# Causal attention: a group's queries and keys loaded in two column halves, each with its own semaphore

## What is computed

```python
xn = _layernorm(x, axis=-1)
s = _L0_attn_ref(xn, ...)          # 16 heads of 16 numbers, causal softmax over all 2048 keys
g = _silu(_L0_ffn_ref(xn, ...))    # two layers with a local window of 128
x = x + s * g
```

```python
scores = jnp.einsum('bhqd,bhkd->bhqk', qc, k) * scale
scores = jnp.where(causal_mask[None, None], -jnp.inf, scores)
m = jnp.max(scores, axis=-1, keepdims=True)
p = jax.nn.softmax(scores - m, axis=-1)
oc = jnp.einsum('bhqk,bhkd->bhqd', p, v)
```

## Time and profile before

| | us |
|---|---|
| median of 3 runs | 4747.14 |
| lowest, highest | 4740.44, 4750.38 |
| the profiled execution's own time | 4743.15 |
| its span, first to last instruction | 4741.2 |
| PE busy | 4448.3 (94%) |
| DVE busy | 3586.0 (76%) |
| ACT busy | 2997.1 (63%) |
| mean granted TensorE clock | 0.972 of full |

### The profile page before, as it was taken

The page is one execution under the profiler, slowest core; times in us unless marked ns, Lnnn a source line. Parts: engine busy times, 40 slices in busy tenths (PEclk is TensorE's granted clock), DMA queues, the critical chain, the costliest instruction groups (busy, mean ns, idle before and its releaser), DMA issues. The chain is left out here.

```text
span 4741.2 us, 92153 instructions
## 1 busy us (share of the span) xinstructions
PE 4448.3 (94%) x32224; PEld 2968.1 (63%) x32224; DVE 3586.0 (76%) x7576; ACT 2997.1 (63%) x6873; POOL 1420.6 (30%) x1940
## 2 busy tenths in 40 slices
PE   8589999999999999699999999999999999999976
PEld 7433443443443433477777777777777777777756
DVE  7488888888888885577777777777777777777736
ACT  3157777777776778366666666665666666666632
POOL 3112222222222122433333334333333333333300
PEclk9789999999999999799999999999999999999999
DMA  8833344433333430200000000010100000000008
GB/s 299 240 45 57 56 90 72 76 59 53 57 64 65 77 65 25 76 23 19 23 15 19 23 19 23 19 50 14 66 20 19 24 19 23 19 23 15 19 13 283
DMA packets 186991, 268.79 MB, mean 57 GB/s; under 512 B 75860, under 2 KB 126764, under 8 KB 179644
## 3 DMA queue, kind: packets, MB, share of 16 engines
q1 hardware_dynamic: 186556, 263.12, 22.5%
HBM read 157.62 MB, written 104.87 MB: 55 GB/s over the span
## 5 line engine op out<-in xcount | busy, mean ns | idle before, releaser
L725 ACT ACTIVATE a_pt<-a_ring 128x512 f32<-128x512 f32 (+3 forms) x2560 | 1180.5, 543 | 438.8 <-PE a_ring L849 421.1
L776 DVE TENSOR_REDUCE a_mx<-a_ring 128x2 f32<-128x1024 f32 (+3 forms) x1079 | 1116.6, 1064 | 244.1 <-PE a_ring L869 118.3
L1136 POOL TENSOR_TENSOR l_rn<-l_ssm,l_half 128x8 f32<-128x8 f32 x256 | 447.8, 1749 | 832.9 <-DVE l_ssm L1386 832.9
L862 PE MATMUL a_ring<-a_ks,a_qs 48*128 48x512 f32 (+3 forms) x2560 | 555.6, 430 | 94.5 <-DMA a_ks<-qk_d 60.9
L849 PE MATMUL a_ring<-a_qs,a_ks 49*128 49x512 f32 (+3 forms) x2560 | 560.2, 445 | 57.9 <-ACT a_pt L725 29.8
L886 PE MATMUL a_ot<-a_pt,a_vt 128*32 128x512 f32 (+3 forms) x5120 | 602.1, 549 | 2.0 <-ACT a_os L731 1.3
L849 PEld LDWEIGHTS a_ring<-a_qs,a_ks 49*128 49x128 f32 x2560 | 248.2, 187 | 464.1 <-ACT a_pt L725 270.8
L1235 ACT ACTIVATE l_pr<-l_pr,l_negm 128x256 f32<-128x256 f32 (+1 forms) x1024 | 501.3, 495 | 7.4 <-DVE l_negm L1438 6.6
L667 POOL TENSOR_TENSOR a_gate<-a_gate 128x1 f32<-128x1 f32 x512 | 99.6, 195 | 1281.4 <-ACT a_pt L725 1271.4
L862 PEld LDWEIGHTS a_ring<-a_ks,a_qs 48*128 48x128 f32 x2560 | 258.1, 191 | 346.2 <-ACT a_pt L725 173.7
L1243 ACT ACTIVATE l_pts<-l_banks 128x512 f32<-128x512 f32 (+1 forms) x512 | 298.6, 583 | 208.7 <-PE l_banks L1705 138.4
(11 more groups left out here) (167 smaller groups left out, 9080.2 us busy)
## 6 DMA issues: line engine op xcount, KB each, us to landing
qk_d<-p_parts SPq DMA_DIRECT2D x16, 2048.0 KB, 10.3
a_qs<-qk_d SPq DMA_DIRECT2D x96, 256.0 KB, 8.3
a_ks<-qk_d SPq DMA_DIRECT2D x96, 256.0 KB, 18.4
l_rot<-rot_s SPq DMA_DIRECT2D x32, 512.0 KB, 4.2
x_d<-l_dx SPq DMA_DIRECT2D x32, 512.0 KB, 2.7
l_xt<-x_d SPq DMA_DIRECT2D x24, 513.0 KB, 5.1
p_x_in<-x SPq DMA_DIRECT2D x16, 512.0 KB, 8.8
x_d<-p_xt SPq DMA_DIRECT2D x16, 512.0 KB, 5.5
```

The lines of the kernel that those rows point to most:

```text
L725: act.activation(pt[:, (g * STEPS + s) % NPT, 2 * piece + f, q0:CHUNK], bank("step", g, k, f)[:, q0:CHUNK], ACT.Exp).then_inc(exp_done.sem, 1)
L776: r = dve.tensor_reduce(mx[:, pr, :, t, kc], ring[:, banks[0]:banks[1] + 1, 0:w], AX.X, ALU.max)
L862: mm = pe.matmul(bank("unit", G, n, f)[:, 0:w], qs[rows, v, pr, q0:q0 + P], ks[rows, v, pr, kc * CHUNK:kc * CHUNK + w], start=True, stop=k ...
L1136: pool.tensor_tensor(out=rn[:, a * HEADS:(a + 1) * HEADS], in0=ssm[:, a * HEADS:(a + 1) * HEADS], in1=half[:, 0:HEADS], op=ALU.pow).then_i ...
```

## The change

Each of the 12 DMAs of `load` becomes two, for columns 0 to 1023 and 1024 to 2047, 128 KB each. All 12 of the first half are issued first, then all 12 of the second, then the values. Each half raises a semaphore of its own. Unit 0 waits for the first half; the first unit of chunk 2, unit 24, waits for the second.

```diff
-        loaded = [tally(f"loaded{u}", 16 * 4 * NSTACK) for u in range(NSLOT)]
+        loaded = [[tally(f"loaded{u}{h}", 16 * 4 * NSTACK) for h in range(2)] for u in range(NSLOT)]
...
                 sp.wait_ge(pv_done.sem, pv_done.at(G - NSLOT))
-                for dst, pick, o in ((qs, STACK_Q, 0), (ks, STACK_K, NGROUP)):
-                    for j, s in enumerate(pick):
-                        for f in range(2):
-                            row = f * HALF + j * A_HD
-                            sp.dma_start(dst[row:row + A_HD, v].bitcast(F32), parts_v[s, f, :, hg + o, :, b])\
-                              .then_inc(loaded[v].sem, 16)
+                for h in range(2):
+                    cols = slice(h * SEQ // 2, (h + 1) * SEQ // 2)
+                    for dst, pick, o in ((qs, STACK_Q, 0), (ks, STACK_K, NGROUP)):
+                        for j, s in enumerate(pick):
+                            for f in range(2):
+                                row = f * HALF + j * A_HD
+                                sp.dma_start(dst[row:row + A_HD, v, :, cols].bitcast(F32),
+                                             parts_v[s, f, :, hg + o, :, b, cols]).then_inc(loaded[v][h].sem, 16)
                 sp.dma_start(v_in[:, v], v_v[:, b, hg]).then_inc(v_loaded[v].sem, 16)
...
-                if n == 0:
-                    pe.wait_ge(loaded[v].sem, loaded[v].per * (G // NSLOT + 1))
+                if n in (0, units.index((CPB // 2, 0, 0, 0))):
+                    half_ = loaded[v][c // (CPB // 2)]
+                    pe.wait_ge(half_.sem, half_.per * (G // NSLOT + 1))
```

## The result

| | before | changed |
|---|---|---|
| median of 5 runs, us | 4747.15 | 4716.7 |
| lowest, highest | 4740.44, 4753.58 | 4708.87, 4722.79 |
| ratio, 95% interval | | 0.9929 (0.9917 to 0.9942) |
| the profiled execution | 4743.15 | 4708.87 |

The kernel is 0.71% faster by the ratio (0.58 to 0.83%), which is some 34 us of 4747; the two medians are 30.5 us apart, and the profiled executions 34.3 us. The forecast was 24.4 us and a time of 4723.

The account below looks back on a forecast made before the run. PE, busy 94% of the span, was taken as the bound, with time to gain only where it idles. 12.5 + 11.9 + 0 = 24.4 us off the median 4747.14 gave 4723 us; range 4711 to 4738.

Parts of the forecast that it names:

- Term 1: First group's load: unit 0 starts once the first half is in, at 212.2 instead of 224.7, 12.5 us earlier.
- The doubt about the rate of 4 KB pieces: First load: whether 4 KB pieces keep the 8 KB rate; 12.5 us gained if bytes count, nothing if cost is by piece.
- The second half in time: First group, unit 24: reached at 232.7 with the second half in at 224.7, 8 us to spare, so no wait.
- Term 2: Later groups' unit 0: all 11 waits for the load go and are given in full, 11.9 us.
- the idle time of the weight loads: Later groups: upper bound of 23.6 us for the gain, if this idle time counts instead of PE's own.
- Term 3: SP's queue behind a load: 12 added issues, 5.5 us, fall inside the 19.78 us in the store; cost 0.
- prologue only: Rival: only the first group's start is gained, PE meets another wait in later groups; 4734.6 us, chance 0.14.
- no change: Rival: the first half isn't in earlier, through shared engines or a fixed cost for each DMA; 4747 us, chance 0.08.
- slower behind a longer load: Rival: 24 DMAs take longer, delaying transfers queued behind; breaks even at 6.0 us longer, 4770 us at 7.5; chance 0.06.

Follow-up runs that it names:

- the run with the first group alone: Against the changed kernel, only the first group's load is halved; later groups load and wait as before: 4738.51 us, ratio 0.9972.
- the quarters' trace: Against the changed kernel, each load in four by chunk, 48 DMAs of 64 KB, four semaphores and waits: 4707.4 us (0.9917), again 4705.21 (0.9909).
- The run with the later groups alone: Against the changed kernel, only the loads of groups 1 to 15 are halved; the first group loads as before: 4731.65 us, ratio 0.9958.
- the load moved ahead: Against the kernel before, whole loads stand ahead of the copy of chunk 2's maxima on SP's queue instead of behind it: 4878.31 us, ratio 1.0269.

## Why the prediction was right

*Term 1, 12.5 us:* right in mechanism, 13.4 measured between the traces and 13 in the run with the first group alone (0.28%). Unit 0 came 0.9 us sooner after the issue than worked out (14.27 instead of 15.2). Half of the 1.2 us by which the whole first load was shorter in 24 DMAs would be 0.6 of that; the rest is not explained. The doubt about the rate of 4 KB pieces settled at the bytes' end. Here the Trainium skill's rule of one fixed cost of about 2 us for each DMA, so that transfers should be as large as possible (SBUF — State Buffer, The DMA setup-cost knee), disagrees with the runs when it is added up over a queue: a load in 24 DMAs was 1.2 us shorter than in 12 in the first group and 2.6 us shorter in the later ones, and 48 of 64 KB moved 139 GB/s. A time of that size is there (2.2 us from issue to landing in the quarters' trace, where the transfers keep up), but the DMAs overlap it.

*The second half in time:* right, unit 24 at 20.57 us with no wait.

*Term 2, 11.9 us:* the waits did go, every one, and the time was given in full: 13.6 us by the table. But the reason given, "with the first half there 12.5 us earlier, all 11 waits go", was not the one at work. They go with one wait for both halves too, because a later load in 24 DMAs is 2.6 us shorter than in 12 and no wait was longer than 1.85. The forecast held the length of a load constant while its number of DMAs doubled. That this error cost nothing is luck: the shorter load and the early half each take away the same waits.

*What the sum left out:* the clock, some 8 to 11 us. The run with the later groups alone gave 20 us for a term of 11.9. The earlier trace rows had a hint: I read the difference of two rounds without a fold, 1.35 us for a wait of 1.01, as the wait alone. I took none of the four rounds with a fold, which were 107.5 to 109.1 us before and 105.4 to 105.8 in three of four in the changed kernel's trace; part of that is chance, since in the other traces without waits such rounds have 105.3 to 108.7. That the missing waits bring part of the gain is shown by where the clock fell and by the load moved ahead. The measured 4716.7 lies in the range only because its lower end, 4711, was taken from the idle time of the weight loads (23.6 us for term 2). The later groups did give some 20 us, but what came on top of term 2 was products at the full clock and not that idle time. The range held for a reason that it did not have, which is luck.

*Term 3, 0:* right as a cost: the added issues took 5.1 us (5.5 expected) out of SP's time in the store, and PE waited for nothing behind it. Wrong was that SP leaves the store at the same distance from the load's start; it left 2.0 us earlier (25.55 instead of 27.59), which is the shorter load again, and the rate of 126 GB/s for the key DMAs was passed too (136 in 201 to 221 us). The run with the load moved ahead shows what it costs when something that PE needs stands in that place.

*The rivals:* "prologue only" is refuted by the run with the later groups alone (0.9958), "no change" by the run with the first group alone, and "slower behind a longer load" never came near its point, since the load became shorter and not longer.

## What to carry to other kernels

Where a stage starts with an idle engine, give the first consumer its own part of the load and its own semaphore: here 13 us for two halves and some 7 to 10 more for four quarters. A wait of a microsecond that recurs each round is a load that is just too late; shortening it a little is as good as waiting for a part, and splitting it into more DMAs can be that little. When a change does two things at once (here a second semaphore and twice the DMAs), run each alone before you say which one worked. Price a recurring wait with what the clock does around it, from several traces, since one trace's time at 1.2 GHz varied by 24 us for the same kernel.

## What the runs showed of the hardware

A load of 3.146 MB into 16 partitions at a time took 27.7 us to its use in the first group as 12 DMAs, 26.5 as 24 cut by columns and 26.8 as 24 cut by head pair; in the later groups it took 28.2, 25.6 and 25.6 us to its last landing. So the size of the pieces made little of it. On SP's queue an issue behind a load of that size and the values in 256-byte rows did not finish for 13 to 20 us, whatever it was: a store (19.78, 12.61) or the maxima (20.13). Which of the two in front holds it up, the load or the values, no run separates. The granted clock of TensorE fell to 1.2 GHz inside each of 14 waits of 5.9 to 8.0 us, and in ten of the 38 waits of 0.06 to 2.62 us within 3 us of their end. Each us at 1.2 GHz cost 0.41 us in this stage.
